# A fused attention and low-rank FFN kernel: split load semaphores, a ring of eight slots, and two buffers of their own

## The reference

```python
q, k, v = x @ Wq, x @ Wk, x @ Wv                       # (4, 8192, 1024)
attn = softmax(where(causal, -inf, q @ k.T) / 32)
x = layernorm(x + (attn @ v) @ Wo)
P = x @ U1                                             # rank 256
H = gelu(P @ V1 + b1)                                  # 4096 wide
x = layernorm(x + (H @ U2) @ V2 + b2)
```

## Time and profile before

| | us |
|---|---|
| median of 2 runs | 2767.18 (2646.22 and 2888.14) |
| the profiled execution | 2540.04 |
| its slowest core, core 1, first to last instruction | 2538.5 |
| the other cores | 2518.9 to 2534.1 |
| TensorE with a matmul in flight, core 1 | 2153.8 |
| DVE / ACT / POOL busy | 771.6 / 662.2 / 353.2 |

### The profile page before, as it was taken

One profiled execution on the slowest core, in us unless ns is written; L12 is line 12 of the kernel. 1 busy time (PEld: TensorE's weight loads), 2 busy tenths in 40 slices (PEclk: granted clock), 3 DMA queues, 4 the chain that ended last, 5 costly groups with the idle time before them and its releaser, 6 DMA issues.

```text
span 2538.5 us, 43117 instructions; the slowest of 8 cores (2518.9 to 2538.5 us)
## 1 busy us (share of the span) xinstructions
PE 2153.8 (85%) x14288; PEld 1351.3 (53%) x14288; DVE 771.6 (30%) x1882; ACT 662.2 (26%) x1389; POOL 353.2 (14%) x653
## 2 busy tenths in 40 slices
PE   0199999999857888898898989898979899898995
PEld 0055455555435555555565656565656566565663
DVE  0034344444335434333314140404040311303104
ACT  0000000000023444334334342424243332423323
POOL 3000111111230010110110202030212112031120
PEclk9999999999978998899898989898989899898997
DMA  9748977796271121232341617170817356192560
GB/s 151 96 77 130 144 169 161 166 174 150 85 140 42 55 67 39 87 121 74 106 138 63 197 54 233 47 239 36 265 63 251 115 172 222 61 294 74 183 221 18
DMA packets 219886, 328.79 MB, mean 130 GB/s; under 512 B 122688, under 2 KB 127824, under 8 KB 218656
## 3 DMA queue, kind: packets, MB, share of 16 engines
q0 software_dynamic: 51120, 166.84, 26.0%
q1 hardware_dynamic: 168560, 159.18, 23.0%
HBM read 287.92 MB, written 77.07 MB: 144 GB/s over the span
## 4 chain that ended last, share of the span: by engine, by line
PE 54%; DVE 7%; ACT 3%; issue 3%; DVEq 3%; POOL 1%; DMA 1%; ACTq 0%; POOLq 0%; SPq 0%
PE ps_s L482 16%; PE ps_a L507 9%; PE ps_a L509 8%; PE ps_x L597 5%; PE ps_a L610 4%; PE ps_a L548 2%; PE ps_s L548 2%; PE ps_s L610 2%; DVE x1t L765 1%; DVEq L790 1%; PE ps_a L482 1%; PE ps_s L629 1%; PE ps_x L532 1%; PE ps_s L532 1%; DVE x L791 1%
## 5 line engine op out<-in xcount | busy, mean ns | idle before, releaser
L646 ACT ACTIVATE p_sb<-ps_s,shift_s 128x256 bf16<-128x256 f32 x512 | 241.4, 474 | 697.4 <-PE ps_s L482 697.2
L482 PE MATMUL ps_s<-qg,kst 128*128 128x256 bf16 x2808 | 363.3, 272 | 2.6 <-DMA kst<-kscr 2.4
L387 POOL DMA_DIRECT2D vst<-vscr x351 | 188.1, 538 | 1104.3 <-PE ps_a L509 1095.7
L482 PEld LDWEIGHTS ps_s<-qg,kst 128*128 128x128 bf16 x2808 | 272.6, 97 | 112.1 <-issue 5.9
L243 PE MATMUL ps_s<-xt,wk_sb 128*128 128x512 bf16 x1024 | 225.6, 381 | 116.2 <-DMA xot<-xobf 116.2
L509 PE MATMUL ps_a<-vst,p_sb 128*128 128x512 bf16 x702 | 264.7, 377 | 0.0
L507 PE MATMUL ps_a<-vst,p_sb 128*128 128x512 bf16 x702 | 264.0, 376 | 0.0
L733 DVE RECIPROCAL recip<-ps_x 128x1 f32<-128x1 f32 x32 | 3.7, 158 | 772.0 <-PE ps_a L509 771.8
L243 PEld LDWEIGHTS ps_s<-xt,wk_sb 128*128 128x128 bf16 x1024 | 100.6, 98 | 235.1 <-issue 118.9
L646 ACT ACT_TABLE_LOAD x30 | 38.5, 1283 | 702.7 <-PE ps_a L482 702.4
L610 PE MATMUL ps_a<-p_sb,v_sb 128*128 128x256 bf16 x704 | 147.6, 311 | 85.2 <-DVE p_sb L807 85.2
(11 more groups left out here) (109 smaller groups left out, 2561.0 us busy)
## 6 DMA issues: line engine op xcount, KB each, us to landing
vst<-vscr POOLq DMA_DIRECT2D x351, 256.0 KB, 4.5
kst<-kscr SPq DMA_DIRECT2D x351, 256.0 KB, 4.7
xbf<-x_seq POOLq DMA_DIRECT2D x16, 1024.0 KB, 12.9
xo<-x_own SPq DMA_DIRECT2D x32, 512.0 KB, 4.2
out<-outb SPq DMA_DIRECT2D x32, 512.0 KB, 3.2
kscr<-kstage POOLq DMA_DIRECT2D x51, 256.0 KB, 4.3
vscr<-vstage POOLq DMA_DIRECT2D x51, 256.0 KB, 3.0
xobf<-x_own POOLq DMA_DIRECT2D x16, 512.0 KB, 15.1
```

Source lines behind the costliest of these rows:

```text
L387: g.dma_start(out=vst[:, slot * 1024:(slot + 1) * 1024], in_=vscr_a[kb - R]).then_inc(vstS[slot], 16)
L482: mm = t.matmul(sbank(kb), k_tile(g_i, kb, dc), qg[:, qb + dc * 256:qb + (dc + 1) * 256], start=(dc == 0), stop=(dc == 7))
L646: sc.activation(p_sb[:, (it % 3) * 256:(it % 3 + 1) * 256], sbank(kb), AF.Exp, bias=shift_s[:, 0:1], scale=SCALE).then_inc(sem_exp, 1)
```

## The change

Three edits.

1. Each of the 8 xt loads of a chunk gets a semaphore of its own, `str_e[tc % 2][ec]`; `str2` counts the 8 xot loads alone. TensorE's wait for the whole chunk is taken away. In the first K accumulation (dco 0) each matmul waits for its slice, and the wait for xot stands between V and Q. The loads, their order and their own waits stay.
2. RING is 8 instead of 9, for K and V. That frees 2 KB of each partition in each ring.
3. Two new tiles, `stT` and `rep_sb`, [128, 512] in float32 (2 KB of each partition each), take the place of columns 1536 to 2047 and 1024 to 1535 of a_sb for the row of statistics and its copies. Instructions, shapes and waits are the same.

```diff
-RING = 9
+RING = 8
+        str_e = [[S(f"se{p}_{e}") for e in range(8)] for p in range(2)]
@@ sync, p1: the loads of xt
-                            transpose=True).then_inc(str2[tc % 2], 16)
+                            transpose=True).then_inc(str_e[tc % 2][ec], 16)
@@ tensor, p1
                 for tc in range(NCHUNK):
-                    t.wait_ge(str2[tc % 2], 256 * (tc // 2 + 1))
                     xb = (tc % 2) * 4096
@@ the K products
                         for ec in range(8):
+                            if dco == 0:
+                                t.wait_ge(str_e[tc % 2][ec], 16 * (tc // 2 + 1))
                             mm = t.matmul(ps_s[u % 2][:, 0:512],
@@ behind the V products, ahead of the Q products
+                    t.wait_ge(str2[tc % 2], 128 * (tc // 2 + 1))
                     for dco in range(8):
@@ p2
+            stT = E2(nc.sbuf_tensor("stT", [128, 512], F32))
+            rep_sb = E2(nc.sbuf_tensor("rep_sb", [128, 512], F32))
@@ tensor, p2 (and the same for columns 1792 to 2048)
                     t.matmul(ps_a[1][:, 0:256], ones_r[0:1, 0:128],
-                             a_sb[0:1, 1536:1792], start=True, stop=True).then_inc(sem_rep, 1)
+                             stT[0:1, 0:256], start=True, stop=True).then_inc(sem_rep, 1)
@@ vector, p2
-                        v.tensor_copy(a_sb[0:1, 1536 + st_i * 128:1536 + (st_i + 1) * 128],
+                        v.tensor_copy(stT[0:1, st_i * 128:(st_i + 1) * 128],
                                       bank[0:1, 0:128])
-                        v.tensor_copy(a_sb[0:1, 1792 + st_i * 128:1792 + (st_i + 1) * 128],
+                        v.tensor_copy(stT[0:1, 256 + st_i * 128:256 + (st_i + 1) * 128],
                                       bank[0:1, 512:640]).then_inc(sem_ste, 1)
-                    v.tensor_copy(a_sb[:, 1024:1280], ps_a[1][:, 0:256])
-                    v.tensor_copy(a_sb[:, 1280:1536], ps_a[1][:, 512:768])
+                    v.tensor_copy(rep_sb[:, 0:256], ps_a[1][:, 0:256])
+                    v.tensor_copy(rep_sb[:, 256:512], ps_a[1][:, 512:768])
```

More of the change, by code:

```diff
@@ L588, in _ @@
                     t.matmul(ps_a[1][:, 0:256], ones_r[0:1, 0:128],
-                             a_sb[0:1, 1536:1792], start=True, stop=True).then_inc(sem_rep, 1)
+                             stT[0:1, 0:256], start=True, stop=True).then_inc(sem_rep, 1)
                     t.matmul(ps_a[1][:, 512:768], ones_r[0:1, 0:128],
-                             a_sb[0:1, 1792:2048], start=True, stop=True).then_inc(sem_rep, 1)
+                             stT[0:1, 256:512], start=True, stop=True).then_inc(sem_rep, 1)
                     def q2_partial(fc):
@@ L804, in _ @@
                                         ps_x[rc][:, 0:256],
-                                        a_sb[:, 1024:1280], ALU.mult)
+                                        rep_sb[:, 0:256], ALU.mult)
                         v.drain()
                         v.scalar_tensor_tensor(p1_sb[:, rc * 256:(rc + 1) * 256],
-                                               a_sb[:, 1280:1536],
+                                               rep_sb[:, 256:512],
                                                u1cs[:, rc:rc + 1],
```

## The result

| | before | after |
|---|---|---|
| median of all runs, us | 2545.25 (26 runs) | 2527.24 (27 runs) |
| lowest, us | 2534.78 | 2516.26 |
| profiled execution: slowest core, span | 2538.5 | 2519.1 |
| profiled execution: mean span of the 8 cores | 2526.9 | 2512.9 |
| ratio | 1 | 0.9944, 95% interval 0.9929 to 0.9959 |

The change saves 0.56% (0.41 to 0.71), about 14 us (10 to 18): faster by more than its measurement is uncertain, and within 2%. The forecast of 2755.0 us was wrong by 228 us. In some executions of either kernel the cores of one die or of both run at a lower granted clock; the ratio leaves these out, the medians in the table contain them, and by their times both runs shown before (2646.22 and 2888.14) were such executions. The same sum on the profiled execution gave 2527.8.

A forecast was written before the change was run, and what follows sets the result against it. The prediction took TensorE's order of work with a long start as the bound. Its terms, -12.2 + 0 + 0, gave 2527.8 us from the profiled 2540.04 and 2755.0 from the two-run median 2767.18; range 2520 to 2880.

The forecast's parts named there:

- What bounds the kernel: Whole kernel: TensorE's own order of work with a long start, 116.2 us of wait before the first K projection.
- Part 1: Start of phase 1: K skips xot and takes xt by slices; V at 119.8 us, 12.2 earlier, slow start of 2.0 included.
- Is the gain kept: Chunks after the start: xot arrives before Q needs it, with about 3 us of room at chunk 1, the tightest place.
- (a): Start: it is not the bound it seems, gain 0, eaten by xot of chunk 1 or the casts; chance 0.10.
- One thing may not shift rigidly: Chunks 4 and 5: casts, stores and transposes crowd the queues; up to 8 us better or worse on the slowest core.
- Part 2: Streamed K and V blocks: a ring of 8 instead of 9 still covers the slowest landing seen; cost 0.
- the rule for the room of a slot: Streamed K: time from issue until wanted is 1.79 us x slots less 4.27 us; 10.0 us with 8 slots.
- (c): Streamed blocks: the ring costs its head start, 20 to 39 us against 12 saved; chance 0.06.
- (d): Streamed blocks: K landings over 10.0 us make every further block wait, 95 us lost at 13 us; chance 0.03.
- Part 3: Statistics row and replicas in own buffers: only addresses move, 0; up to 10 us either way if addresses were worse.
- The sum and the number given: Whole kernel: -12.2 + 0 + 0, giving 2527.8 us profiled and 2755.0 on the median of the two runs.
- (e): Whole kernel: the time moves by what the runs differ in, 2528 to 2650 us or up to 2876; chance 0.12.

The follow-up runs named there:

- e2: The kernel before with the first edit alone (ring of 9, no new buffers): ratio to before 0.9943, 14.5 us faster.
- e3: The changed kernel, with the first K product of a chunk waiting for all eight xt slices: ratio to before 0.9951.
- e5: The changed kernel with two extra unused matmuls behind each of the first seven slice waits of chunk 0: ratio to before 0.9921.
- e9: The changed kernel with four staging buffers for V instead of two: ratio to before 0.9948.
- e12: The changed kernel without the casts of chunks 3 to 15, their loads rereading chunks 0 to 2 (outputs no result): ratio to before 0.9932.
- e8: The changed kernel with GpSimd's first loads reordered: casts of chunk 0, K, V, Q weights, casts of chunks 1 and 2, small tables: ratio to before 0.9905.

## Why the prediction was right or wrong

**What bounds the kernel**: right. It is TensorE's order of work with a start that waits for DMA; e2 and e3 move the start, and the end moves with it.

**Part 1**: right in mechanism and size. Last slice at 106.08 (105.5 predicted), V 14.24 us later (14.3), slow start paid again (taken 2.0; e5 shows 1.7 us in the means). The first Q matmul came 11.2 us earlier over the cores, 12.2 predicted: before's cores had their own last xot landing between 114.0 and 116.2, and 12.2 was worked out from core 1, the latest. The finer waits cost nothing that can be seen: the body of phase 1 is 534.9 us on average and 531.2 on the fastest core before, 534.8 and 531.2 after. For the 0.01 to 0.1 us that the prediction's upper bound gave a wait, no run has a measurement.

**Is the gain kept**: yes, as the prediction had it. There is no wait for xot on any core, and (a) is refuted.

**"One thing may not shift rigidly"**: right that it is there, too small. I gave up to 8 us. The body of phase 1 has a floor of 531.2 us and cost a core up to 11 us in before, 24 in e2 and 34 in e9. I put it down to "the casts, stores and transposes" together; in e12, without most of the casts, it is gone.

**Part 2**: right. Cost 0, and the rule for the room of a slot gave the size of the loss for 5 slots (0 to 35, measured 20) and, with the luck named above, for 4 (100, measured 105). It was too careful at 6: "8 slots still cover the slowest landing seen, by 0.9 us" asks more than is needed: at 6 slots the median of 4.7 had 1.8 us of room, and nothing was lost. What (c) and (d) describe begins at 5 slots, not at 8.

**Part 3**: right. The copies and products keep their durations, for instance the copy into a_sb on core 1 of before and that into rep_sb on core 3 of after:

```profile
L796 DVE COPY a_sb<-ps_a x16: 424/424/425, 751.8 to 2498.5; 128x256 f32<-128x256 f32 x16
...
L801 DVE COPY rep_sb<-ps_a x16: 424/424/425, 739.1 to 2480.0; 128x256 f32<-128x256 f32 x16
```

**The sum and the number given**: here is the step that failed. "The median of the two runs shown is 2767.18 us [...] 2767.18 - 12.2 = 2755.0." The sum was made against 2540.04 and gave 2527.8; the measured median is 2527.24. That the two agree to 0.6 us is luck: 2540.04 is 5.2 us under the measured median of before, 2545.25, and the medians differ by 18.0 us and not 12.2. From there I moved the sum by the difference between the profiled execution and two runs that were 9% apart, although the profile gave no work in which those 106 to 348 us could lie. In place of the 2767.18 us that it took as the base, before's 26 runs have a median of 2545.25, and 18 of them lie between 2534.78 and 2549.63; the two runs shown are among the other 8 (2600.17 to 2888.14). The rival (e), with a chance of 0.12, had foreseen this, and the time is 0.8 us under its 2528 to 2650. The execution with all eight cores within 20 us of each other was the better base for the number. The saving itself, 12.2 us, lies within the measured 10 to 18, and the forecast of a change within 2% was right.

## What to carry to other kernels

When a wait stands for several transfers, ask which of them its next work reads, and move the others' wait down to their reader. Here that brought 9.4 us, for a semaphore of their own and a moved wait; waiting for each slice brought another 1.8. For the depth of a ring, compare the room (slots x block period, less the time from use to reissue) with the median landing: here 6.5 us against 4.7 cost nothing, 4.7 against 4.6 cost 20 us, and nothing between was tried; slots beyond that are memory for nothing. Where SyncE's small transposes share the DMA engines with a long queue of casts, hold the casts that aren't needed yet, rather than issue everything as early as possible (13.8 us here, and 44 us against before with the first loads in order of need and four staging buffers).

## What the runs showed of the hardware

- A transposing load landed in 2.5 to 4.0 us with no packets of GpSimd's queue under way (xot of chunk 0 in before). Behind casting DMAs on GpSimd's queue it took 28.4 us in before, and in e8 the slices came 6 us apart and then after a gap of 35 us.
- In stretches in which both queues had work, they moved nearly equal numbers of packets, whatever the size: 48 and 48 in before (80 to 90 us, 1.05 MB of casts against 0.01 MB of transposes), 2733 and 2737 in e8 (36 to 96 us). So large packets on one queue held up a queue of small ones.
- With the casts of three chunks instead of sixteen the body of phase 1 was equal to 0.1 us on eight cores (e12), so TensorE's own pace is that steady there.
- A wait taken away by more buffers came back at the next transfer in the same crowd (e9, core 5: 0.2 us at Q, 29.4 us at xt).
- TensorE's lower level after idling (weight loads 0.43 us apart against 0.22) was not left by seven matmuls spread over 7 us (after), and was left while matmuls ran back to back (e5, after 102.93). The granted clock in the rows read 1.00 at either spacing.
